# First attention: values as the stationary operand in quarters of the array, sums by products with ones

## The reference

```python
q = (x @ Wq).reshape(b, n, 32, 8)              # x here is the layer norm of x
k, v = jnp.split(ctx @ Wkv, 2, axis=-1)        # each reshaped to 32 heads of 8
q = apply_axial_rope(q, pos_map)
k = apply_axial_rope(k, ctx_pos_map)
logits = jnp.einsum('bqhd,bkhd->bhqk', q, k) * scale
w = jax.nn.softmax(logits, axis=-1)
attn = jnp.einsum('bhqk,bkhd->bqhd', w, v)
return attn.reshape(b, n, 256) @ Wout + bout
```

## Time and profile before

| what | value |
|---|---|
| median of 3 runs | 985.07 us (979.59 to 987.73) |
| profiled execution, its own time | 979.97 us |
| its span, first to last instruction | 978.2 us |
| mean granted TensorE clock | 0.954 |
| TensorE, matmul busy | 839.0 us (86%) |
| VectorE busy | 672.4 us (69%) |
| ScalarE busy | 432.5 us (44%) |
| GpSimd busy | 334.4 us (34%) |

### The profile page before, as it was taken

The page is one execution under the profiler, slowest core; times in us unless marked ns, Lnnn a source line. Parts: engine busy times, 40 slices in busy tenths (PEclk is TensorE's granted clock), DMA queues, the critical chain, the costliest instruction groups (busy, mean ns, idle before and its releaser), DMA issues. The chain is left out here.

```text
span 978.2 us, 25958 instructions
## 1 busy us (share of the span) xinstructions
PE 839.0 (86%) x9368; PEld 643.6 (66%) x9368; DVE 672.4 (69%) x1587; ACT 432.5 (44%) x1029; POOL 334.4 (34%) x292
## 2 busy tenths in 40 slices
PE   4799999999998899999889999999997840288882
PEld 2577787777777789989756666666665730155551
DVE  5778878787787665655377777777775589455661
ACT  2344444344444423323456666666666750032230
POOL 3434444344343050000134343433342110347763
PEclk9899999999999999999999999999999775599997
DMA  7420000000000000000001111111110399865542
GB/s 227 127 70 18 11 16 13 13 16 11 16 16 28 2 12 0 0 0 0 3 17 29 32 32 32 32 32 30 32 31 23 125 350 276 197 155 92 93 70 33
DMA packets 62075, 56.61 MB, mean 58 GB/s; under 512 B 24016, under 2 KB 57168, under 8 KB 62032
## 3 DMA queue, kind: packets, MB, share of 16 engines
q1 hardware_dynamic: 55888, 46.61, 16.7%
q0 software_dynamic: 6144, 9.44, 5.6%
HBM read 41.81 MB, written 14.22 MB: 57 GB/s over the span
## 5 line engine op out<-in xcount | busy, mean ns | idle before, releaser
L421 ACT ACTIVATE pr_t<-bank 128x512 f32<-128x512 f32 x128 | 76.4, 597 | 148.1 <-PE bank L314 147.4
L858 POOL TENSOR_TENSOR g_k_bd<-g_k_t,head_mask 128x1024 f32<-128x1024 f32 x32 | 60.6, 1893 | 123.9 <-ACT g_k_t L1037 123.9
L314 PE MATMUL bank<-ident,sub 128*128 128x128 f32 x512 | 82.4, 284 | 2.7 <-ACT pr_t L421 2.1
L314 PEld LDWEIGHTS bank<-ident,sub 128*128 128x128 f32 x512 | 56.7, 141 | 29.6 <-issue 17.4
L513 DVE TENSOR_TENSOR sub<-bank,top 128x2048 f32<-128x2048 f32 x32 | 73.3, 2292 | 3.9
L276 POOL TENSOR_TENSOR rot<-part_a,part_b 128x512 f32<-128x512 f32 x32 | 40.9, 1278 | 99.8 <-DVE part_b L524 99.8
L682 ACT ACTIVATE f_hid<-bank,b 128x128 f32<-128x128 f32 x128 | 36.5, 368 | 85.6 <-PE bank L628 85.5
L509 DVE TENSOR_REDUCE top<-bank 128x32 f32<-128x2048 f32 x32 | 73.1, 2284 | 0.4 <-PE bank L302 0.3
L853 POOL TENSOR_TENSOR xres<-xres,g_out_bias 128x256 f32 (+1 forms) x32 | 23.5, 734 | 142.4 <-DVE g_xn L1061 142.4
L326 PEld LDWEIGHTS bank<-v_bd,pr_t 128*64 128x64 f32 x2048 | 64.9, 138 | 10.7 <-issue 10.7
L326 PE MATMUL bank<-v_bd,pr_t 128*64 128x18 f32 x2048 | 71.3, 213 | 0.0
(11 more groups left out here) (203 smaller groups left out, 2007.9 us busy)
## 6 DMA issues: line engine op xcount, KB each, us to landing
e_w_gu<-in_experts_in SPq DMA_DIRECT2D x11, 768.0 KB, 8.4
table<-r_row SPq DMA_DIRECT2D x16, 320.0 KB, 7.1
e_w_d<-in_experts_out SPq DMA_DIRECT2D x11, 384.0 KB, 10.2
out<-xres SPq DMA_DIRECT2D x32, 128.0 KB, 1.7
xres<-in_x SPq DMA_DIRECT2D x2, 1152.0 KB, 10.3
xres<-in_experts_in SPq DMA_DIRECT2D x3, 768.0 KB, 20.5
keys_in<-in_ctx_t SPq DMA_DIRECT2D x32, 64.0 KB, 1.8
vals_in<-in_ctx_t SPq DMA_DIRECT2D x32, 64.0 KB, 1.8
```

Source lines behind the costliest of these rows:

```text
L314: m = pe.transpose(b_pr[:, j * P:(j + 1) * P], sub[:, v, cols], k.ident[:, :])
L421: act.activation(pr_t[:, e, :, :].rearrange("p j q -> p (j q)"), b_pr[:, :], ACT.Exp).then_inc(a_exp, 1)
L858: pool.tensor_tensor(k_bd[:, v, :, :, :, :].rearrange("p c b h s -> p (c b) h s"), k_t[:, v, :, :].rearrange("p c (b a s) -> p (c b) a s", ...
```

## The change

In `values` the roles are exchanged. The values of a pair of heads on their block diagonal, now 32 columns wide (`VW0 = 4 * HD0`: 16 for the pair and 16 zeros, behind the pair for f = 0 and ahead of it for f = 1), are the stationary operand and take one quarter of the array's columns (32 partitions of the output); the exponents of one batch, 64 columns, move. Two parts e = 2c and 2c + 1 add into the same 32 partitions of column block c of the bank, each with its 16 rows (f = 0 or 1). The sums come from products of a stationary block of ones (`ones`, 32 columns, ones for the own head's eight columns) with the moving exponents of both batches, 128 columns, into columns 256 to 511 of the same bank: each sum appears on the eight partitions of its head. So `b_o` holds the attended rows already turned (features on partitions, queries in columns) and beside them their sums in the same shape. VectorE takes the reciprocal of 256 columns in place of 32, and its multiplication writes `att_t` directly. The tile `att`, the two transposes, ScalarE's copy to `att_t` and the semaphores a_attT and a_attTc go. The output projection's two products move from behind the key projection to where the transposes stood. The residual addition and bn_stats of tile f move ahead of the rotary multiplications. The value projection writes its columns in another order (by halves f), and the weights `first_v_w` and `first_out_w` are reordered on the host.

```diff
-VW0 = 2 * HD0 + 2
+VW0 = 4 * HD0
+HALF0 = 2 * (NHP0 // 2) * VW0
...
-        v_bd = z.sb("v_bd", [P, 2, 2, NHP0, VW0])
-        rcp = z.sb("rcp", [P, H0])
-        att = z.sb("att", [P, 2, D])
+        v_bd = z.sb("v_bd", [P, 2, 2, HALF0 + 2 * HD0])
+        ones = z.sb("ones", [P, 2, VW0])
+        rcp = z.sb("rcp", [P, D])
...
-            pool.memset(v_bd[:, :, :, :, :], 0.0).then_inc(a_fill, 1)
-            pool.wait_ge(a_fill, 2)
+            pool.memset(v_bd[:, :, :, :], 0.0).then_inc(a_fill, 1)
+            pool.memset(ones[:, :, :], 0.0).then_inc(a_fill, 1)
+            pool.wait_ge(a_fill, 3)
             for h in range(2):
-                pool.memset(v_bd[64 * h:64 * h + 64, :, :, :, 2 * HD0 + h:2 * HD0 + h + 1], 1.0).then_inc(a_fill, 1)
+                for f in range(2):
+                    first = 2 * HD0 * f + HD0 * h
+                    pool.memset(ones[64 * h:64 * h + 64, f, first:first + HD0], 1.0).then_inc(a_fill, 1)
...
+            both_halves = v_bd[:, :, :, :].rearrange("p u f w -> p u (f w)")
...
+                c, f = e // 2, e % 2
+                for b in range(2):
+                    for j in range(4):
+                        hp = 8 * (j // 2) + 2 * e + j % 2
+                        first = (b * NHP0 // 2 + 2 * (hp // 4) + hp % 2) * VW0
+                        pe.matmul(b_o[32 * j:32 * j + 32, c * P + b * S:c * P + (b + 1) * S],
+                                  both_halves[:, v, f * HALF0 + first:f * HALF0 + first + VW0], pr_t[:, e, j, b * S:(b + 1) * S],
+                                  start=(e == 0 and b == 0), stop=False)
                 for j in range(4):
-                    hp = 8 * (j // 2) + 2 * e + j % 2
-                    for b in range(2):
-                        m = pe.matmul(b_o[64 * b:64 * b + 64, hp * VW0:(hp + 1) * VW0], pr_t[:, e, j, b * S:(b + 1) * S],
-                                      v_bd[:, v, b, hp, :], start=True, stop=True)
+                    m = pe.matmul(b_o[32 * j:32 * j + 32, D + c * P:D + (c + 1) * P], ones[:, f, :], pr_t[:, e, j, :],
+                                  start=False, stop=(e == 3))
...
                     for c in range(KC):
-                        m = pe.transpose(b_turn[:, c * P:(c + 1) * P], att[:, u, c * P:(c + 1) * P], k.ident[:, :])
-                    m.then_inc(a_attT, 1)
+                        m = pe.matmul(b_turn[:, D:2 * D], att_t[:, u, c, :], wo[:, c, :], start=(c == 0), stop=(c == KC - 1))
+                    m.then_inc(a_out, 1)
...
-                if on[4]:
-                    pe.wait_ge(a_attTc, f + 1)
-                    for c in range(KC):
-                        m = pe.matmul(b_turn[:, D:2 * D], att_t[:, u, c, :], wo[:, c, :], start=(c == 0), stop=(c == KC - 1))
-                    m.then_inc(a_out, 1)
...
-                if on[4]:
-                    act.wait_ge(a_attT, f + 1)
-                    if later(f, 2):
-                        act.wait_ge(a_out, f - 1)
-                    act.activation(att_t[:, u, :, :].rearrange("p c q -> p (c q)"), b_turn[:, 0:D],
-                                   ACT.Copy).then_inc(a_attTc, 1)
-                if on[3]:
                     exps(3)
...
+                if on[4]:
+                    dve.wait_ge(a_out, f + 1)
+                    dve.wait_ge(a_bias, f + 1)
+                    dve.tensor_tensor(tile_of(k.xres, f), b_turn[:, D:2 * D], tile_of(k.xres, f), ALU.add).then_inc(a_x1, 1)
+                if on[4]:
+                    dve.wait_ge(a_x1, f + 1)
+                    dve.bn_stats(tile_of(k.raw, f), tile_of(k.xres, f)).then_inc(a_raw1, 1)
...
                 if on[3]:
-                    o3 = b_o[:, 0:NHP0 * VW0].rearrange("p (n w) -> p n w", w=VW0)
                     dve.wait_ge(a_pv, w + 1)
-                    dve.reciprocal(rcp[:, :].rearrange("p (n h) -> p n h", h=2), o3[:, :, 2 * HD0:VW0]).then_inc(a_rcp, 1)
...
+                    dve.reciprocal(rcp[:, :], b_o[:, D:2 * D]).then_inc(a_rcp, 1)
                     dve.wait_ge(a_rcp, w + 1)
                     if later(w, 2):
-                        dve.wait_ge(a_attT, w - 1)
-                    dve.tensor_tensor(att[:, v, :].rearrange("p (n h d) -> p n h d", n=NHP0, h=2),
...
+                        dve.wait_ge(a_out, w - 1)
+                    dve.tensor_tensor(att_t[:, v, :, :].rearrange("p c q -> p (c q)"), b_o[:, 0:D], rcp[:, :],
                                       ALU.mult).then_inc(a_att, 1)
```

More of the change, by code:

```diff
@@ L195, in first_attention @@
          a_xnT, a_xnTc, a_qk, a_rope, a_rot, a_rotT, a_qkt, a_kbd, a_v, a_vbd, a_s, a_top, a_sub,
-         a_prT, a_exp, a_pv, a_rcp, a_att, a_attT, a_attTc, a_out, a_bias, a_x1, a_raw1
+         a_prT, a_exp, a_pv, a_rcp, a_att, a_out, a_bias, a_x1, a_raw1
          ) = z.sems(
@@ L200, in first_attention @@
              "a_xnT a_xnTc a_qk a_rope a_rot a_rotT a_qkt a_kbd a_v a_vbd a_s a_top a_sub "
-             "a_prT a_exp a_pv a_rcp a_att a_attT a_attTc a_out a_bias a_x1 a_raw1")
+             "a_prT a_exp a_pv a_rcp a_att a_out a_bias a_x1 a_raw1")
         x_in, keys_done, vals_done = [a_xin0, a_xin1, a_xin2, a_xin3], [a_keys0, a_keys1], [a_vals0, a_vals1]
@@ L214, in first_attention @@
                    (wv[:, :, :].rearrange("p h m -> p (h m)"), ins["first_v_w"]),
-                   (wo[:, :, :], ins["L0_xattn_Wout"].rearrange("(c p) n -> p c n", p=P)),
+                   (wo[:, :, :], ins["first_out_w"].rearrange("(c p) n -> p c n", p=P)),
                    (bo[:, :], over_rows(ins["L0_xattn_bout"]))]
@@ L359, in step @@
                         for h in range(2):
-                            m = pe.matmul(b_qk[64 * h:64 * h + 64, b * P:(b + 1) * P], vals_in[:, u, b * S:(b + 1) * S],
-                                          wv[:, h, :], start=True, stop=True)
+                            m = pe.matmul(b_qk[64 * h:64 * h + 64, 0:D].rearrange("p (f b m) -> p b f m", f=2, b=2)[:, b],
+                                          vals_in[:, u, b * S:(b + 1) * S], wv[:, h, :], start=True, stop=True)
                     m.then_inc(a_v, 1)
@@ L406, in scalar @@
             act.preload_act_table_set("natural_log_exp_and_others")
-            act.wait_ge(a_fill, 4)
+            act.wait_ge(a_fill, 7)
             row_scales(act, k, EARLY_X_SUMS, first_x)
@@ L444, in step @@
                         rows = slice(64 * h, 64 * h + 64)
-                        act.activation(v_bd[rows, u, :, :, h * HD0:(h + 1) * HD0].rearrange("p b n d -> p (b n) d"),
-                                       b_qk[rows, 0:D].rearrange("p (m d) -> p m d", d=HD0), ACT.Copy).then_inc(a_vbd, 1)
+                        act.activation(v_bd[rows, u, :, 0:HALF0].rearrange("p f (m w) -> p f m w", w=VW0)[:, :, :, h * HD0:(h + 1) * HD0],
+                                       b_qk[rows, 0:D].rearrange("p (f m d) -> p f m d", f=2, d=HD0), ACT.Copy).then_inc(a_vbd, 1)
                 if on[3]:
                     exps(2)
-                if on[4]:
-                    act.wait_ge(a_attT, f + 1)
-                    if later(f, 2):
-                        act.wait_ge(a_out, f - 1)
-                    act.activation(att_t[:, u, :, :].rearrange("p c q -> p (c q)"), b_turn[:, 0:D],
-                                   ACT.Copy).then_inc(a_attTc, 1)
-                if on[3]:
                     exps(3)
@@ L526, in step @@
                                           ALU.mult).then_inc(a_rope, 1)
[L527 to L530, removed]
                 if on[3]:
-                    o3 = b_o[:, 0:NHP0 * VW0].rearrange("p (n w) -> p n w", w=VW0)
                     dve.wait_ge(a_pv, w + 1)
-                    dve.reciprocal(rcp[:, :].rearrange("p (n h) -> p n h", h=2), o3[:, :, 2 * HD0:VW0]).then_inc(a_rcp, 1)
[L535 to L538, removed]
+                    dve.reciprocal(rcp[:, :], b_o[:, D:2 * D]).then_inc(a_rcp, 1)
                     dve.wait_ge(a_rcp, w + 1)
                     if later(w, 2):
-                        dve.wait_ge(a_attT, w - 1)
-                    dve.tensor_tensor(att[:, v, :].rearrange("p (n h d) -> p n h d", n=NHP0, h=2),
-                                      o3[:, :, 0:2 * HD0].rearrange("p n (h d) -> p n h d", h=2),
-                                      rcp[:, :].rearrange("p (n h a) -> p n h a", h=2, a=1).to_broadcast([P, NHP0, 2, HD0]),
+                        dve.wait_ge(a_out, w - 1)
+                    dve.tensor_tensor(att_t[:, v, :, :].rearrange("p c q -> p (c q)"), b_o[:, 0:D], rcp[:, :],
                                       ALU.mult).then_inc(a_att, 1)
@@ L1927, in lay_out @@
     laid["pos_rows"] = np.ascontiguousarray(a["fside_BxSx2_0"].reshape(NT, P, 2).transpose(1, 0, 2))
-    laid["first_v_w"] = by_parity(a["L0_xattn_Wkv"][:, D:2 * D], HD0)
+    pairs = by_parity(a["L0_xattn_Wkv"][:, D:2 * D], HD0).reshape(C, 2, NHP0 // 4, 2, 2, HD0)
+    laid["first_v_w"] = np.ascontiguousarray(pairs.transpose(0, 1, 3, 2, 4, 5)).reshape(C, D)
+    quarters = np.asarray(laid.pop("L0_xattn_Wout")).reshape(2, 2, 2, 2, 2 * HD0, D)
```

(1 more changed line is left out.)

## The result

The kernel after takes 999.78 us (median of 4 runs, 997.16 to 1002.78) against 983.84 for the kernel before (4 runs): ratio 1.0164, 95% interval 1.011 to 1.0218. It is slower by 16 us; forecast was +22, at 1007. The profiled execution took 1002.78 us, span 1001.0.

A forecast was written before the change was run, and what follows sets the result against it. TensorE sets the pace, with VectorE's chain to xn the tight place. Per step +1.44 - 0.47 - 0.10 = +0.87 us, over 28 steps +24.4, drain -2.4: +22.0, so 1007 us as a median, range 992 to 1032.

The forecast's parts named there:

- the forecast's own 1000 to 1016: Whole kernel: the main case's own range around 1007 us, given a chance of 0.70.
- The reciprocal: On VectorE, growing from 128x32 to 128x256: 1.80 us, from 152 ns fixed and 6.43 ns an element.
- The rival with 2.86 us: VectorE's reciprocal dearer, 11.2 ns an element, up to 1037 us in all, half way 1022; chance 0.07.
- the one with 0.40: VectorE's reciprocal streams like a multiplication, xn is not late, each step gains 0.57 us, 967 in all; chance 0.06.
- The delay of L342: TensorE's transposes of xn wait for VectorE behind the long reciprocal: 1.44 us later in each step having both.
- The 0.06 for a later last product: Last product into the bank has 128 columns in place of 18 and ends some 0.06 us later.
- Turned rows and wo: On TensorE two transposes go and wo products take their place: gain 0.47 us a step.
- The products: TensorE's values and ones products in rounds of four: 1.86 us a tile against 2.01, gain taken as 0.1.
- The rival with 31 ns an instruction: TensorE's 96 products cost by instruction count, adding 1.07 us to all 32 tiles, about 1041 us; chance 0.10.
- the one with broken rounds: Products adding into the same bank run as two, not four: +1.9 us a tile, over 1055 us; chance 0.03.
- No bound by VectorE: VectorE's work rises from 7.4 to 8.8 us a step, under what the step becomes.
- the drain and the end: Last steps without xn: two gain 1.4 us each, the last reciprocal stands open for 0.4, together -2.4.

The follow-up runs named there:

- e4: The changed kernel with VectorE's loop over steps 4 to 31 written out, other engines keeping their loops: 997.41 us, ratio 1.0153 to the kernel before.
- e9: The kernel of e7 with the output projection's products moved back behind the key projection: 982.0 us, ratio 0.9979 to the kernel before.
- e2: The kernel before with one more reciprocal, 128x256, into a scratch tile ahead of the small one: 1035.49 us in one run.
- e5: The changed kernel with VectorE making xn of the next tile before the reciprocal and att_t of the last one: 980.7 us, ratio 0.9959 to the kernel before.
- e7: The changed kernel with the reciprocal on ScalarE as exp(-ln(sum)) and xn ahead of att_t on VectorE: 965.3 us, ratio 0.981 to the kernel before.

## Why the prediction was right

The forecast was 1007 in 992 to 1032 and slower with a chance of 0.89; 999.78 is in the range and just under the forecast's own 1000 to 1016. Point by point:

- **The reciprocal.** 1.80 us forecast, 1758 ns measured. The two small rows carried over a factor of 8: 32 and 256 elements give (1758 - 358) / 224 = 6.25 ns an element and 158 ns fixed, against 6.43 and 152. The rival with 2.86 us and the one with 0.40 are out.
- **The delay of L342.** Forecast +1.44 us. Over the 22 steady steps it is 2.86 us from the scores to L354 in the mean against 1.57 to L342 before: +1.28. Errors in both directions partly cancel. att_t starts 0.04 us after the reciprocal's end, not 0.14 as I took from sub. The 0.06 for a later last product did not come: the reciprocal starts 0.10 to 0.13 us after the next scores, and before it was 0.11. And in every other step the loop's end adds (e4), which I had left out.
- **Turned rows and wo.** Forecast -0.47, measured -0.57 between third and fourth turn (209.81 to 211.97 against 207.11 to 209.85). What goes beyond the forecast lies in the query products: 0.86 us to the key products in place of 0.97. e9 shows that the place counts.
- **The products.** Forecast -0.10, measured +0.09, the one term with the wrong sign. The pace inside the parts was right: 0.22 to 0.25 us for sixteen values products and 0.22 for eight with ones, 0.44 to 0.47 a part. The rival with 31 ns an instruction would have made it 0.74, the one with broken rounds 0.9; both are out. What I sized wrong are the gaps between tile shapes. Where a product of another tile shape follows (the value projection behind part 0, the scores behind part 3), the ones take 0.36 and 0.35 us to it in place of 0.22. Part 0 therefore takes 0.61 us in place of 0.49, parts 1 to 3 take 1.48 against 1.51.
- **Not forecast:** -0.17 between L354 and the first values products (1.24 us against 1.41). Before, the second turn waited there for ScalarE's Exp; now Exp has ended while TensorE waits for xn. Together 1.28 - 0.57 + 0.09 - 0.17 = +0.63, with 0.01 elsewhere the 0.64 measured, against the forecast's 0.87.
- **No bound by VectorE.** It is busy 45.46 of 50 us. e2 shows a delay without that bound, and e5 the bound itself at 48.01 of 50.
- **The sum in the profiled execution** fits by luck: 1002.0 forecast, 1002.78 measured. From the first reciprocal over 28 steps it is +19.3 us where 24.4 was forecast. For the drain and the end, forecast at -2.4, it is -1.8 to the last reciprocal, and then the long reciprocal at the very end and the clock (below) add 3.5 until f_ys of the feed forward is first written. Ahead of the first reciprocal it was 1.0 sooner. That makes 344.9 to 364.9, +20. The untouched part from there to the end adds 2.8: it lasts between 633 and 638 us in the eleven profiles of this case, 633.3 before and 636.1 after.
- **The total.** Against the medians the change is +16 where +22 was forecast. The term that was too large is the steady step: 0.87 in place of 0.64 us, 6 us over 28 steps. The delay of L342 was 0.16 shorter than forecast, the turned rows gave 0.10 more and 0.17 wasn't forecast at all, against 0.19 that the products cost more. The other 1.2 us between 1007 and 999.78 are the median before, which one more run moved from 985.07 to 983.84.

## What to carry to other kernels

When operands are exchanged so that a result comes out turned, look at what becomes wide: the sums here were copied over eight partitions and the reciprocal's free size grew from 32 to 256, at 6.25 ns an element. Then ask who stands behind it in the engine's order; xn had nothing to do with the reciprocal and was held by it. Give the long operation to an idle engine and put independent work ahead of it: that turned +16 us into -18 (e7).

## What the runs showed that was not expected

TensorE's clock fell at both ends of the stage. In the windows of the kernel after (busy of the five engines, then granted clock), a wait of 2.66 us for the first xn behind the late row statistics, and one of 1.98 us for the last att_t, are each followed by a stretch at a mean of 0.59 of the full clock, largely at the lower level of 1.2 GHz:

```profile
42.00:46.30 4.30, 1.64 (x37) 0.95 (x37) 3.51 (x10) 1.03 (x3) 0.76 (x2) 1.00 0.00 0
46.30:50.50 4.20, 4.20 (x45) 3.16 (x46) 4.17 (x2) 1.96 (x4) 2.62 (x2) 0.59 0.00 0
...
347.00:349.50 2.50, 0.53 (x10) 0.19 (x2) 2.23 (x3) 0.00 (x0) 0.00 (x0) 1.00 0.03 10
349.50:357.00 7.50, 6.84 (x27) 5.93 (x28) 5.97 (x31) 2.54 (x5) 0.00 (x0) 0.59 0.00 0
```

In the kernel before, where the waits at these places are 1.24 us and at most 0.70, it stays at 1.00:

```profile
45.80:48.00 2.20, 2.13 (x34) 1.96 (x34) 2.20 (x2) 1.47 (x3) 1.27 (x2) 1.00 0.00 0
330.00:336.00 6.00, 4.27 (x47) 3.32 (x45) 5.07 (x24) 1.04 (x3) 0.00 (x0) 1.00 0.02 4
336.00:341.00 5.00, 5.00 (x45) 4.89 (x44) 4.00 (x21) 3.52 (x10) 0.00 (x0) 1.00 0.00 0
```

The first interval between reciprocals is 2.3 us longer than before. From L354 to L384 in it, behind the wait, it is 4.40 us (46.27 to 50.67) in place of the 2.95 of a steady step. The eight products L648 behind the last wait take 1.97 us in place of 1.00. Through the steady steps, each with a wait of 1.0 to 1.3 us, the granted clock is 1.00.

The kernel before has a stretch of its own at the lower level, earlier: the granted clock is 0.53 from 37.80 to 41.40 us. There TensorE had waited for keys_in (L384 below). In the kernel after the same wait was shorter, the clock stayed at 1.00 behind it, and the same products (L396) took 1.13 us in place of 2.08:

```profile
37.80:41.40 3.60, 3.55 (x10) 2.74 (x10) 0.92 (x3) 0.00 (x0) 0.00 (x0) 0.53 0.46 134
```

```profile
37.85 2.08 PE L384 MATMUL bank<-wq,xn_t 128*128 128x256 f32 x4 [1.65 <-DMA keys_in<-in_ctx_t]
```

```profile
38.51 1.13 PE L396 MATMUL bank<-wq,xn_t 128*128 128x256 f32 x4 [1.38 <-DMA keys_in<-in_ctx_t]
```

So in these two executions part of what the kernel after loses to the clock behind the first xn was lost by the kernel before at another place.
